# A state-space mixer on one core: carried and within-block products of two head pairs side by side, with fixed roles for four PSUM banks

## What is computed

```python
h = x * rsqrt(mean(x * x) + EPS) * norm_w
proj = einsum('bsd,od->bso', h, in_proj_w)          # gate, hidden + B + C, dt
gate, hBC, dt = split(proj)
hBC = silu(causal_conv(hBC, conv_w, conv_b))        # 4 taps
hid, B, C = split(hBC)
dt = softplus(dt + dt_bias);  A_full = -exp(A_log) * dt
# blocks of 128 positions
M = einsum('bcihn,bcjhn->bcijh', Ch, Bh) * L        # L = exp of the decay from j to i, lower triangle
Y_diag = einsum('bcijh,bcjhp->bcihp', M, hid * dt)  # within a block
states = einsum('bclhn,bhcl,bclhp->bchpn', Bh, decay_states, hid * dt)
Y_off = einsum('bclhn,bchpn,bhcl->bclhp', Ch, carried_states, exp(A_cs))
y = Y_diag + Y_off + Dp * hid
yg = y * silu(gate);  yg = yg * rsqrt(mean over the group of yg**2 + EPS) * gnorm_w
out = x + einsum('bsd,od->bso', yg, out_proj_w)
```

## Time and profile before

| | us |
|---|---|
| median of 3 runs | 2010.82 |
| lowest, highest | 2008.63, 2013.45 |
| the profiled execution | 2008.87 |
| its span, first to last instruction | 2007.1 |
| TensorE busy | 1952.2 (97%) |
| VectorE busy | 1594.6 (79%) |
| ScalarE busy | 1483.1 (74%) |
| GpSimd busy | 1230.5 (61%) |

### The profile page before, as it was taken

The page is one execution under the profiler, slowest core; times in us unless marked ns, Lnnn a source line. Parts: engine busy times, 40 slices in busy tenths (PEclk is TensorE's granted clock), DMA queues, the critical chain, the costliest instruction groups (busy, mean ns, idle before and its releaser), DMA issues.

```text
span 2007.1 us, 32870 instructions
## 1 busy us (share of the span) xinstructions
PE 1952.2 (97%) x10906; PEld 1573.0 (78%) x10906; DVE 1594.6 (79%) x2979; ACT 1483.1 (74%) x2986; POOL 1230.5 (61%) x853
## 2 busy tenths in 40 slices
PE   7998999999999999999999999999999999999998
PEld 6564666777888888888888888888888888888877
DVE  7777899857877878878778787878787878787888
ACT  5245866547787878787878787878787878787776
POOL 5644777544656666666656656565666565666666
...
GB/s 202 192 51 148 100 93 85 157 147 134 132 93 132 93 132 107 125 116 124 121 107 119 105 119 109 115 125 112 122 116 109 116 111 113 156 118 107 135 96 122
DMA packets 114473, 241.75 MB, mean 120 GB/s; under 512 B 23681, under 2 KB 24706, under 8 KB 113794
## 3 DMA queue, kind: packets, MB, share of 16 engines
...
## 4 chain that ended last, share of the span: by engine, by line
PE 76%; DVE 2%; ACT 1%; issue 0%; DVEq 0%; ACTq 0%
PE s_ps L74 13%; PE s_ps L76 13%; PE s_ps L75 13%; PE s_ps L1861 6%; PE s_ps_o L74 6%; PE s_ps_o L76 6%; PE s_ps_o L75 6%; PE s_ps L1827 5%; PE s_ps L1869 4%; PE s_ps L1819 3%; DVE s_cv L2100 1%; PE s_ps L1845 1%; PE s_ps L1805 1%; PE s_ps L1811 0%; DVE s_state L2076 0%
## 5 line engine op out<-in xcount | busy, mean ns | idle before, releaser
L2278 POOL TENSOR_TENSOR w_lo<-w_raw,w_hi 128x1024 fp32r<-128x1024 f32 x142 | 340.0, 2401 | 534.7 <-ACT w_hi L1932 534.7
L74 PE MATMUL s_ps<-h_hi,w_hi 128*128 128x512 f32 x1152 | 463.0, 402 | 6.2 <-DVE s_hid L2105 4.6
L76 PE MATMUL s_ps<-h_hi,w_lo 128*128 128x512 f32 x1152 | 450.2, 391 | 0.0
L75 PE MATMUL s_ps<-h_lo,w_hi 128*128 128x512 f32 x1152 | 448.6, 389 | 0.0
L2100 DVE SCALAR_TENSOR_TENSOR s_cv<-s_ps,s_par,s_cv 128x511 f32<-128x511 f32 (+2 forms) x480 | 355.9, 744 | 15.5 <-ACT s_cv L1975 9.7
L2295 POOL TENSOR_TENSOR s_lm<-s_lm,s_cbt 128x512 f32<-128x512 f32 x256 | 326.8, 1301 | 12.5 <-ACT s_lm L1957 12.5
L1950 ACT ACTIVATE s_lm<-s_rows,s_steps 128x128 f32<-128x128 f32 x1024 | 312.4, 390 | 2.0 <-PE s_ps L1861 2.0
L1975 ACT ACTIVATE s_cv<-s_ps,s_par 128x512 f32<-128x512 f32 x160 | 124.5, 778 | 221.7 <-PE s_ps L76 221.7
L74 PEld LDWEIGHTS s_ps<-h_hi,w_hi 128*128 128x128 f32 x1152 | 216.5, 188 | 53.1 <-DVE s_hid L2105 5.8
L76 PEld LDWEIGHTS s_ps<-h_hi,w_lo 128*128 128x128 f32 x1152 | 216.2, 188 | 47.5
L75 PEld LDWEIGHTS s_ps<-h_lo,w_hi 128*128 128x128 f32 x1152 | 216.9, 188 | 41.0
...
## 6 DMA issues: line engine op xcount, KB each, us to landing
...
s_wo_raw<-in_w_out SPq DMA_DIRECT2D x128, 256.0 KB, 3.7
...
```

The lines of the kernel that those rows point to most:

```text
L74: nc.tensor.matmul(dst, l_hi, r_hi, start=start, stop=False)
L75: nc.tensor.matmul(dst, l_hi, r_lo, start=False, stop=False)
L76: return nc.tensor.matmul(dst, l_lo, r_hi, start=False, stop=stop)
L2278: nc.gpsimd.tensor_tensor(w_lo[:, slot, :], w_raw[:, slot, :], w_hi[:, slot, :].bitcast(F32), ALU.subtract).then_inc(w_lo_ready, 1)
```

## The change

The eight slots of a unit become four **doubles** s of two pairs a = 2s and b = 2s + 1. `slot_jobs` gives way to three written lists: `first_jobs` (before the first unit), `double_jobs(s)` and `last_jobs` (the last unit), which name the bank of each job. In a double TensorE does OFF(a), OFF(b), DIAG(a), DIAG(b), T, G(a), H(a), G(b), T, H(b), ST, ST, OP(a), OP(b). The banks are A (DIAG(a), H(a), in s=1 also C's projection), B (DIAG(b), H(b)), C (OFF(a), T, ST of the even pair, CB or BT) and D (OFF(b), G, ST of the odd pair, in s=1 B's projection, in s=3 SQ). States and transposes are made two pairs ahead for both pairs; a unit now does its own OP of the last pair. The carried product of an odd pair goes to `s_tg`. C and B are projected in s=1 (`BC_SLOT` is 4). SQ is four transposes of `s_ssq`, summed by a VectorE tensor_reduce, at the end of the unit instead of in the next one, and the square root takes scale and bias with it. The orders of ScalarE, VectorE, GpSimd and SP are written anew (`act_double`, `dve_double`, `pool_double`, `sp_double`).

```diff
+def double_jobs(s):
+    a, b = 2 * s, 2 * s + 1
+    jobs = [(C_BANK, ("OFF", 0, a)), (D_BANK, ("OFF", 0, b)), (A_BANK, ("DIAG", 0, a)), (B_BANK, ("DIAG", 0, b)),
+            (C_BANK, ("T", *divmod(a + 2, KC))), (D_BANK, ("G", 1, a)), (A_BANK, ("H", 1, tile_of(a)))]
+    if s == 2:
+        jobs += [(C_BANK, ("CB", 1, 0))]
+    if s == 3:
+        jobs += [(C_BANK, ("BT", 1, 0))]
+    jobs += [(D_BANK, ("G", 1, b)), (C_BANK, ("T", *divmod(b + 2, KC))), (B_BANK, ("H", 1, tile_of(b))),
+             (C_BANK, ("ST", *divmod(a + 2, KC)))]
+    if s == 3:
+        jobs += [(D_BANK, ("SQ", 0, 0)), (None, ("OP", 0, a)), (D_BANK, ("ST", *divmod(b + 2, KC)))]
+    else:
+        jobs += [(D_BANK, ("ST", *divmod(b + 2, KC)))]
+        if s == 1:
+            jobs += [(A_BANK, ("H", 1, C_AT)), (D_BANK, ("H", 1, B_AT))]
+        jobs += [(None, ("OP", 0, a))]
+    return jobs + [(None, ("OP", 0, b))]
...
+        def act_double(act, un, s):
...
+            act_w(act, *load_unit(un, EARLY[s]))
+            act_wo(act, un, a)
+            act_diff(act, ua, 2 * a_on)
+            act_y(act, un, a)
+            act_sq(act, un, a)
+            act_wo(act, un, b)
+            act.wait_ge(y_chain, (un.u * KC + b) * 2 + 2)
+            act_gate(act, v, a, bank(un, ("G", 1, a)))
+            act_y(act, un, b)
+            act_sq(act, un, b)
+            act_diff(act, ua, 2 * a_on + 1)
+            act_tap(act, v, tile_of(a), h_a)
+            if s == 1:
+                act_w(act, v, LOADS.index(("BC", 0)))
+            act_exps(act, ua, a_on)
+            act_gate(act, v, b, bank(un, ("G", 1, b)))
+            if s:
+                act_tanh(act, v, tile_of(a), h_a)
+            act_diff(act, ub, 2 * b_on)
+            act_diff(act, ub, 2 * b_on + 1)
+            act_tap(act, v, tile_of(b), h_b)
...
+            act_exps(act, ub, b_on)
+            act_scale(act, ua, a_on)
+            if s == 1:
+                act_tap(act, v, C_AT, bank(un, ("H", 1, C_AT)))
+            else:
+                act_scale(act, ub, b_on)
+            if s == 3:
+                act_rms(act, un)
+            if load_unit(un, LATE[s]):
+                act_w(act, *load_unit(un, LATE[s]))
+            act_tanh(act, v, tile_of(b), h_b)
+            if s == 1:
+                act_scale(act, ub, b_on)
+                act_tap(act, v, B_AT, bank(un, ("H", 1, B_AT)))
+                act_tanh(act, v, C_AT, bank(un, ("H", 1, C_AT)))
+                act_tanh(act, v, B_AT, bank(un, ("H", 1, B_AT)))
...
+        def dve_double(dve, un, s):
...
+            dve_yoff(dve, un, a)
+            dve_yoff(dve, un, b)
+            dve_y_skip(dve, un, a)
+            dve_y_carried(dve, un, a)
+            dve_y_gated(dve, un, a)
+            dve_y_skip(dve, un, b)
+            dve_y_carried(dve, un, b)
+            dve_y_lo(dve, un, a)
+            dve_y_gated(dve, un, b)
...
+            state(0)
...
+            if s == 3:
+                dve_ssq(dve, un, bank(un, ("SQ", 0, 0)))
+            state(1)
+            if s == 1:
+                dve_skip(dve, v)
+            dve_tile(dve, v, tile_of(b), h[1])
+            if s == 1:
+                c_bank, b_bank = bank(un, ("H", 1, C_AT)), bank(un, ("H", 1, B_AT))
+                dve_silu(dve, v, tile_of(b), h[1])
+                dve_tile(dve, v, C_AT, c_bank)
+                dve_conv(dve, v, B_AT, b_bank, 1)
+                dve_silu(dve, v, C_AT, c_bank)
+                dve_conv(dve, v, B_AT, b_bank, 2)
+                dve_conv(dve, v, B_AT, b_bank, 3)
+                dve_silu(dve, v, B_AT, b_bank)
+            else:
+                dve_silu(dve, v, tile_of(b), h[1])
```

More of the change, by code:

```diff
@@ L1779, in sp_unit, with sp_end @@
+        def sp_end(sp, un):
+            for k in range(2, KC):
+                if k + 2 < KC:
+                    sp_rows(sp, un, k + 2)
+                sp_wo(sp, un, k)
+                if k == 2:
                     sp_back_g(sp, 0)
[L1780 removed]
+                if k == 4:
                     sp_back_x1(sp, 0)
@@ L2153, in dve_out, with carried @@
                 dve_out_tile(dve, v, t)
+        def carried(un, k):
+            return tg[:, 0:3 * P] if k % 2 and not un.last else yoff[:]
         def dve_yoff(dve, un, k):
@@ L2324, in pool_unit, with pool_end, schedule @@
+        def pool_end(pool, un):
+            for k in range(KC):
+                if 2 <= k + 1 < KC:
+                    pool_m(pool, un, k + 1)
+                pool_wo(pool, un, k)
+                if k == 1:
+                    pool_product(pool, 0, 0)
+                if k and k != KC - 1:
+                    pool_sum(pool, un, k)
+                if 2 <= k < 1 + TB:
                     pool_product(pool, 0, k - 1)
-        def schedule(eng, unit, end):
-            unit(eng, Unit(-1, 1))
+        def schedule(eng, first, unit, last):
+            first(eng, Unit(-1, 1))
@@ L2332, in schedule, with doubles, unit @@
                 unit(eng, Unit(g + 1, 0))
-            unit(eng, Unit(GROUPS - 1, 1, last=True))
-            if end:
-                end(eng)
+            last(eng, Unit(GROUPS - 1, 1, last=True))
+        def doubles(double):
+            def unit(eng, un):
+                for s in range(PAIRS):
+                    double(eng, un, s)
+            return unit
         with nc.Block() as block:
```

547 lines of the change are left out of this document (309 added, 238 removed).

## The result

The changed kernel took 2042.05 us (median, 2040.25 to 2043.92), beside 2009.74 (2008.63 to 2013.45) for the kernel before on the same chip: 1.016 times as long, 95% interval 1.0147 to 1.0172. The prediction was 2012, with a range of 1986 to 2034. The profiled execution has a span of 2039.2 us, 32.1 more than before.

What follows compares the result with a forecast made beforehand. TensorE, busy all 97.57 us of a unit, was taken as the bound. Its savings and three new waits, -26 + 7 + 12 + 8 = +1 us against the profiled 2008.87, gave 2012 us by the median; range 1986 to 2034.

Steps and rivals of the forecast that it cites:

- What the change takes off TensorE: TensorE's own work in the units: fewer changes into and out of DIAG, cheaper SQ, one stall gone; 1.7 us per unit saved.
- First wait: In each double H(a) needs DIAG(a)'s bank just as y_lo(a) frees it: 0.12 per double, 60 times, 7 us.
- Second wait: After the double with C and B, OFF(b) waits for bT to free bank D: 0.8, 15 times, 12 us.
- Skip 0.08: VectorE's instruction making the skip weights, in its work leading to bT's silu: put at 0.08 us.
- Third wait: In s=3 ST(b) behind OP(a) delays VectorE, so the next double's H(a) is 0.55 later: 15 times, 8 us.
- covered with 0.2 to spare: In s=3, ScalarE's two table loads were to leave its tanh ready at 23.8, before the convolutions at 23.95.
- The drain on top of each table load: The skill's rule of about 1380 ns more per load; if right, 2.8 us per unit, some 40 us in all.
- Both together 0, between -4 and 4: Start, where OFF(0) waits about 2 us for the last silu, and end, where OP(0) waits for y_lo: no net cost.
- The other edits cost nothing: GpSimd streams, ScalarE's order, SP's DMAs and SQ's reduce were all taken as covered, adding no time.
- The clock falls: Rival, 3%: the stall behind bT drops TensorE's clock once per unit, 15 x 1.6 = 24 us: 2036.
- The chain is longer: Rival, 24%: each of six links from DIAG(a) to y_lo(a) takes 0.05 more, paid 60 times, 18 us: 2030.
- grouping saves nothing: Rival, 6%: DIAG's cost lies in every group, so the 0.3 saved per double doesn't come: 2018.

Runs made afterwards that it cites:

- skip_on_act: The changed kernel with the 4x skip weights computed by ScalarE ahead of the tap of C and no longer by VectorE: 2030.8 us, ratio 1.0106.
- sq_late: The changed kernel with ST(b) straight behind ST(a) in s=3 and SQ in bank C between the two OPs, summed between convolutions: 2038.6 us, ratio 1.0136.
- sq_late_tanh: sq_late with ScalarE's weight split moved behind the last tanh of the fourth double: 2026.7 us, ratio 1.0099.
- start_moved: The changed kernel with ScalarE's exponentials, scales and tap and VectorE's states reordered in the first schedule alone: 2034.4 us, ratio 1.012.
- best_a: combined with OFF(b)'s scaling between pair a's skip and carried step, last sums spread, and the first schedule's last four banks changed: 2004.2 us, ratio 0.9994.
- combined: The changed kernel with OFF(a), DIAG(a), OFF(b), DIAG(b) in each double, plus the edits of skip_on_act and start_moved: 2016.0 us, ratio 1.0033.
- grouped_all: best_a plus sq_late_tanh's fourth double, with OFF(a), OFF(b), DIAG(a), DIAG(b) and both scalings ahead of the skip again: 2009.8 us, against 2002.3 ungrouped.

## Why the prediction was wrong

**What the change takes off TensorE**: right. A unit after holds 3.06 us of waits and restarts (four at H(a), one at OFF(b), below), so without them 98.63 - 3.06 = 95.57, 2.0 less than before; the prediction said 1.7.

**First wait (H(a) for y_lo(a))**: mechanism and chain right, 6.65 measured for 6.61, and y_lo seen 4.08 after DIAG(a) for 4.06. The term was too small. It took a release that is just late to cost 0.12 in all; it cost 0.15 of wait and 0.11 of restart, since the matmul was due at 1016.50, 6.56 after OFF(a), and not at 6.66. 0.26 a double instead of 0.12. The aside that y_lo had "until the second next DIAG" before is wrong, though no sum rests on it: DIAG had only bank B, so it was the next one, at 1029.99, for a y_lo made at 1027.40.

**Second wait (OFF(b) for bT)**: mechanism right, size not: 1.51 with its restart (1.41 start to start and 0.10 in the rows behind), for 0.8. The step that failed is "Skip 0.08", for which the prediction names no row; before, the instruction took 0.16. Here it takes 1.07, and skip_on_act showed that it is on the path: without it the loss is 0.8, as forecast.

**Third wait (the last double)**: right to 0.1. H(a) there loses 0.77 in all, for 0.12 + 0.55. sq_late and sq_late_tanh bear out both halves, ST(b) behind OP(a), and right behind it the table loads, which were "covered with 0.2 to spare": with the states early they are the limit. The drain on top of each table load (the Trainium skill, ScalarE: Activation LUTs, section What ACT_TABLE_LOAD costs) isn't in any row: the next instruction begins 0.02 behind the load to the root (1082.60 + 1.28, 1083.90), and in sq_late 0.01 behind the load back (1188.40 + 1.28, 1189.69).

These three were 1.83 us a unit in the prediction and are 3.06: the sum of a unit is +1.05 instead of +0.1. In the 15 units that run doubles that is 16 us of the 32, where the prediction had 1.

**"Both together 0, between -4 and 4"** is the step that failed most: the start cost 12.3 (0.69 of it is work that moved there). The prediction looked at the last wait alone (2 us, measured 2.01), and not at how the exponentials, now needed sooner, stand ahead of the gate in ScalarE's order and the states ahead of the tile in VectorE's. Two waits of 2.8 us and two stretches at the lower clock, 4.4, came of it. start_moved took some 6 of the 12.1 us off the start, and best_a's banks 1.6 to 3.3 more (61.2 in combined, 57.9 to 59.6 in the four runs with these banks).

**"The other edits cost nothing"**: unit 14's pairs of sums cost 2.6, which the prediction didn't mention. Unit 0 and the last unit together have 2.9 more, of which about 1 is the unit's usual 1.05. In the last unit a term is missing from the prediction, the wait of 2.67 for `s_yoff` behind the other two sums; the clock of 0.57 behind it comes on top. What each is worth by itself wasn't tried.

**The rivals.** "The clock falls" (3%, 2036) came nearest in size, but not in kind: in the mixer the lower clock came at the start and in the last unit only; in units 1 to 14 waits of up to 1.42 us kept the full clock (1.00 from 592 to 1975 us), as forecast. "The chain is longer" (24%, 2030) wasn't it either: the chain was as forecast. That grouping saves nothing is refuted for TensorE's own time; for the kernel grouping is worse than that, it costs 7.4 us, as grouped_all shows.
